# State space loop of a two-layer decoder: where a batch's x is transposed and where its y is gated

## What is computed

```python
zxbcdt = x @ W_in.T                       # z 512, xBC 768, dt 64
xBC = silu(causal_conv(xBC, conv_w))      # 4 taps
dt = softplus(dt_raw + dt_bias);  a = dt * -exp(A_log);  cum = cumsum(a)
M  = (C B^T) * exp(cum_i - cum_j) * dt_j  # lower triangle, 64 heads
y  = M @ xs + D * xs                      # 512 columns
yz = y * silu(z)                          # the gate
out = (yz * rsqrt(mean(yz^2) + eps) * norm_w) @ W_out.T
```

## Time and profile before

| | |
|---|---|
| median of 3 runs | 2280.41 us (2278.93 to 2284.31) |
| the profiled execution | 2281.86 us, its span 2279.9 us |
| busy share of the span: PE, DVE, ACT, POOL | 90%, 73%, 58%, 55% |
| state space stage | from about 923 us to 1370 us of the span |

### The profile page before, as it was taken

How to read it: one execution, slowest core, us unless ns; L and a number is a source line. 1 busy time by engine, 2 the same in 40 slices (tenths; PEclk the granted TensorE clock), 3 DMA queues, 4 the chain that set the end, 5 groups by cost and what they waited for, 6 DMA issues and landing times.

```text
span 2279.9 us, 35595 instructions
## 1 busy us (share of the span) xinstructions
PE 2049.1 (90%) x10116; PEld 1339.3 (59%) x10116; DVE 1663.0 (73%) x3833; ACT 1330.4 (58%) x5022; POOL 1256.0 (55%) x1508
## 2 busy tenths in 40 slices
PE   7889999999999996698989985999999999999996
PEld 5646666566665663455555542666666666666664
DVE  7755666676666765688887764777878788878886
ACT  3655666666666664233333224777777777777773
POOL 0153444544445431377766662667676777777775
PEclk9989999999999999799999987999999999999998
DMA  6000000000000010100000002000000000000000
GB/s 214 1 19 3 3 4 2 5 2 2 2 2 5 0 56 23 66 19 19 19 19 10 1 0 81 3 4 6 6 6 7 6 5 6 5 6 5 6 3 8
DMA packets 30094, 37.61 MB, mean 16 GB/s; under 512 B 3329, under 2 KB 24321, under 8 KB 29313
## 3 DMA queue, kind: packets, MB, share of 16 engines
q1 hardware_dynamic: 29952, 36.11, 4.8%
HBM read 34.00 MB, written 2.10 MB: 16 GB/s over the span
## 4 chain that ended last, share of the span: by engine, by line
PE 66%; DVE 12%; ACT 12%; issue 7%; POOL 3%; DMA 0%; DVEq 0%; SPq 0%; POOLq 0%; ACTq 0%
PE xa_pJB L715 5%; PE xa_pS L734 5%; PE ssm_pX L1289 5%; PE fa_pJB L1774 5%; PE xa_pO L808 5%; PE xa_pY L838 5%; PE xa_pJA L715 4%; PE fa_pS L1793 4%; PE ssm_pL L1283 3%; PE fa_pY L1824 3%; PE fa_pJA L1754 3%; PE fa_pO L1811 3%; PE fa_pH L1875 2%; DVE ssm_y L1532 2%; PE fa_pJB L1754 2%
## 5 line engine op out<-in xcount | busy, mean ns | idle before, releaser
L1242 POOL TENSOR_TENSOR ssm_y<-ssm_y,ssm_term 128x512 f32<-128x512 f32 x112 | 141.9, 1267 | 120.8 <-DVE ssm_term L1485 118.5
L1710 POOL TENSOR_TENSOR fa_rs<-fa_rs,all_minus_half 128x4 f32<-128x4 f32 x192 | 198.2, 1032 | 15.1
L1901 ACT ACTIVATE fa_qT<-fa_pH,all_fa_head_vec 128x512 f32<-128x512 f32 x128 | 99.5, 777 | 172.3 <-PE fa_pH L1875 172.3
L1910 ACT ACTIVATE fa_pS<-fa_pS,fa_nb 128x128 f32<-128x128 f32 x512 | 182.6, 392 | 7.2 <-issue 6.8
L1707 POOL TENSOR_TENSOR fa_rs<-fa_ms,all_eps5w 128x4 f32<-128x4 f32 x192 | 43.9, 229 | 240.0 <-ACT fa_q_junk L1894 132.3
L1793 PEld LDWEIGHTS fa_pS<-fa_kT,fa_qT 128*128 128x128 f32 x1024 | 124.7, 192 | 65.3 <-ACT fa_qT L1901 58.5
L1733 POOL TENSOR_TENSOR fa_cat<-fa_ov,fa_om 128x512 bf16<-128x512 f32 x128 | 153.7, 1201 | 5.3
L667 POOL TENSOR_TENSOR xa_rs<-xa_ms,all_eps 128x4 f32<-128x4 f32 (+1 forms) x65 | 13.1, 201 | 259.3 <-ACT xa_junk L882 259.3
L1793 PE MATMUL fa_pS<-fa_kT,fa_qT 128*128 128x128 f32 x1024 | 149.1, 289 | 2.4 <-ACT fa_qT L1901 0.9
L1724 POOL TENSOR_TENSOR fa_ov<-fa_ob,fa_om 128x512 f32<-128x512 bf16 x128 | 147.8, 1154 | 4.7 <-DVE fa_om L2088 4.7
L734 PE MATMUL xa_pS<-all_shared_weights,xa_qT 128*128 128x256 f32 x512 | 125.8, 387 | 23.3 <-ACT all_shared_weights L913 17.5
(11 more groups left out here) (327 smaller groups left out, 5944.3 us busy)
## 6 DMA issues: line engine op xcount, KB each, us to landing
all_shared_weights<-in_fa_w SPq DMA_DIRECT2D x12, 512.0 KB, 3.8
fa_cat<-in_fa_wproj SPq DMA_DIRECT2D x8, 512.0 KB, 3.8
all_shared_weights<-in_xa_wq SPq DMA_DIRECT2D x1, 2048.0 KB, 14.0
xa_wo<-in_xa_wo SPq DMA_DIRECT2D x1, 2048.0 KB, 18.8
xa_ctxT<-in_ctxT SPq DMA_DIRECT2D x16, 128.0 KB, 2.1
all_shared_weights<-in_fa_wkvx SPq DMA_DIRECT2D x1, 2048.0 KB, 8.7
fa_ctxT<-in_ctxT SPq DMA_DIRECT2D x16, 128.0 KB, 2.1
out_x<-all_X SPq DMA_DIRECT2D x16, 128.0 KB, 1.7
```

The lines of the kernel that those rows point to most:

```text
L1710: pool.tensor_tensor(rs[:, j % 2, cols], rs[:, j % 2, cols], env.mhalf[:, cols], ALU.pow)\
L1910: last = act.activation(four(pS[j % 2])[:, i, :], four(pS[j % 2])[:, i, :], ACT.Exp, bias=nb[:, j % 2, i:i + 1], accum_out=rsum[:, j % 2, ...
```

## The change

Four moves, all in `state_space`.

- PE: the transposes of x of batch m+1 are issued in step m, behind the last tap and ahead of the spans matmuls. Batch 0's are issued ahead of the wait for the stage's weights.
- ACT: the copy to `xT` of batch m+1 is issued in step m, between the silu of xs and the exp of the decays. Batch 0's is issued ahead of the steps.
- DVE: the gate of batch m-1 is issued in step m, behind term 6, with a wait for the POOL addition of level 6; before, it was the first instruction of step m+1.
- DVE: the residual (1517) has a further wait, for the normalised x of the batch before.

```diff
     def tensor(pe):
+        def transpose_x(b):
+
+            pe.wait_ge(s["z_in"], now(b, 0))
+            for k in range(KT):
+                last = pe.transpose(pZ[:, k * P:(k + 1) * P], env.X[:, b, k * P:(k + 1) * P], env.ident[:])
+            last.then_inc(s["xT_ps"], 1)
+
...
             if front:
-                pe.wait_ge(s["z_in"], now(m, 0))
-                for k in range(KT):
-                    last = pe.transpose(pZ[:, k * P:(k + 1) * P], env.X[:, m, k * P:(k + 1) * P], env.ident[:])
-                last.then_inc(s["xT_ps"], 1)
                 pe.wait_ge(s["xT_in"], now(m + 1, 0))
...
             if front:
                 last.then_inc(s["xs_ps"], 1)
+                if m + 1 < B:
+                    transpose_x(m + 1)
                 pe.wait_ge(s["a_done"], now(m + 1, 0))
...
         env.xa_stage.left(pe)
+        transpose_x(0)
         pe.wait_ge(w_ready, 1)
...
+        def copy_x(b):
+
+            act.wait_ge(s["xT_ps"], now(b + 1, 0))
+            act.activation(xT[:, :, PAD:PAD + P], pZ[:, 0:D].rearrange("p (k c) -> p k c", k=KT),
+                           ACT.Copy).then_inc(s["xT_in"], 1)
+
...
             if front:
-                act.wait_ge(s["xT_ps"], now(m + 1, 0))
-                act.activation(xT[:, :, PAD:PAD + P], pZ[:, 0:D].rearrange("p (k c) -> p k c", k=KT),
-                               ACT.Copy).then_inc(s["xT_in"], 1)
...
                 act.activation(xs[:], pX[:, :], ACT.Silu).then_inc(s["xs_in"], 1)
+                if m + 1 < B:
+                    copy_x(m + 1)
                 act.wait_ge(s["dec_ps"], now(m + 1, 0))
...
         act.wait_ge(pad_in, 1)
+        copy_x(0)
         sequences(act, steps)
...
-            if back:
-                dve.wait_ge(y_added, now(m - 1, 0, LEVELS, LEVELS - 1))
-                dve.tensor_tensor(y[:, 1 - side, :], y[:, 1 - side, :], sz[:, 1 - side, :], ALU.mult)\
-                    .then_inc(s["gated"], 1)
             if front:
...
                 dve.wait_ge(s["rms_done"], now(m - 1, 0))
+                dve.wait_ge(norm.x_done, now(m - 1, 0) - 1)
...
             terms(6)
+            if attend:
+                dve.wait_ge(y_added, now(m, 0, LEVELS, LEVELS - 1))
+                dve.tensor_tensor(y[:, side, :], y[:, side, :], sz[:, side, :], ALU.mult).then_inc(s["gated"], 1)
             if front:
```

## The result

The changed kernel takes 2274.68 us (median of 16 runs, 2271.67 to 2278.80) against 2281.09 us (16 runs): 6.4 us less, ratio 0.9973 with a 95% interval of 0.9965 to 0.998. So it is faster, by 4.6 to 8.0 us. The forecast was 4.8 us less. The execution that the profile shows took 2278.80 us, its span 2276.9; it is the slowest of the 16, and its state space stage begins 2.5 us later than in the profile before, for reasons that lie ahead of the stage.

What follows compares the result with a forecast made beforehand. The prediction took the ACT, DVE, ACT, PE loop of each state space batch as the bound. Copies +5.70, gates -7.80 and -0.86, start and end terms gave -4.76 us: 2280.41 - 4.8 = 2275.6, range 2272.2 to 2280.2.

Steps and rivals of the forecast that it cites:

- The loop: State space batch, from decays ready to the next decays ready: ACT to DVE, DVE, ACT, PE sets its time.
- Part 1, the gate: DVE: moving the gate takes 0.60 us a batch out of the loop; xdt, blocked by skip, ends at 1132.97.
- with nothing to spare: DVE against ACT: blocked xdt, ending at 1132.97, is just covered by dec, ready at 1132.98.
- Part 2, the copy: ACT: the copy to xT pushes table load and dec by 0.38 us a batch and buys nothing.
- the sum: Whole change: 5.70 - 7.80 - 0.86 + 0.27 - 0.60 - 0.87 - 0.60 = -4.76 us.
- 7.80 - 0.86: DVE: 13 gates at 0.60 us save 7.80; the first gate, stuck behind a POOL centring, saves 0.86.
- Part 3, the start: Batch 0 on PE: dt starts at most 1.20 us earlier, at half clock, taken as 0.60 us saved.
- The terms at the end: Stage end on DVE: batch 14's gate -0.60, batch 15's gate -0.87, late xdt in batch 15 +0.27 us.
- The second rival: POOL's power operation holds the gate on DVE, 15 x 0.32 = 4.8 us, gain gone, 2280.4; chance 0.15.
- The third: PE clock: rises after the same work, another 0.60, and a fall costing 1.6 vanishes, -7.0 us, 2273.4; chance 0.17.
- The fourth: PE clock falls behind the new stop ahead of level 2, 1.6 us each, +6.4 us, 2286.8; chance 0.06.

Runs made afterwards that it cites:

- runs 10 to 12: Second profiles of the kernel before, the changed kernel, and the kernel with the gate moved and skip on DVE: 2280.61, 2275.06 and 2272.73 us.
- run 2: Only the gate moved against the kernel before, x transposed and copied in its own step: 2274.77 us, ratio 0.9971.
- run 4: Full change plus, in the gate's old place on DVE, a multiply of the same size that nobody reads: 2290.25 us, ratio 1.0037 to the kernel before.
- run 5: Kernel before with the gate moved and skip computed on DVE behind xdt instead of on POOL, x as before: 2271.31 us, ratio 0.9957.
- runs 1 and 4: Run 1: only x transposed and copied ahead, gate left in its old place, 2288.40 us, ratio 1.0032 to the kernel before; run 4 has its own line.

## Why the prediction was right

**The loop** was right and was what decided. All experiments gave the steady batch that it asks for within 0.04 us, down to 25.23, once the copy's 0.27 and the late `xdt`'s 0.29 were known from the changed kernel. The prediction itself asked for 0.22 less a batch; it was 0.32.

**Part 1, the gate.** 0.60 out of the loop, as worked out. `xdt` blocked by `skip`, as worked out: it was to end 2.22 behind the last addition (1132.97 against 1130.75) and did so by 2.20 (1133.34 against 1131.14). The margin "with nothing to spare" turned out the other way round by 0.08: `xdt` comes last, behind `dec`, and holds `xd`.

**Part 2, the copy.** The mechanism was right (in ACT's way, buys nothing), the term mis-sized. I counted its duration, 0.38; it moves the table load and `dec` by 0.27, since it starts 0.10 ahead of the end of xs, 1131.04 against 1131.14, where a table load doesn't. That is the term that was off: the sum has 15 x 0.38 = +5.70, and with the blocked `xdt` as the true releaser it is 15 x 0.29 = +4.35. The difference of 1.35 us takes the forecast from -4.8 to -6.1. The stage without its costly falls of the clock is 6.0 and 6.1 us shorter in the two pairs of profiles (runs 10 to 12), and the stretch between the first and the last xs alone is 4.3 and 4.2 us shorter, where 4.35 - 7.80 - 0.86 gives -4.31. I had seen from the rows that both delays are of one size, but not that this makes the copy's half of the change worthless: with the gate alone the 0.29 is paid as well.

**Part 3, the start.** From the stage's first DVE instruction to the first xs 24.35 us before and 24.15 after, in the second pair 24.33 and 23.72: -0.2 and -0.6. The forecast had -0.60. dt does start 1.24 us earlier in the stage, as against the 1.20 worked out, and the B and C part of batch 0 takes 6.0 to 6.4 us now instead of 5.4, since more of it is done at half speed. The granted clock rises 13.4 us into the stage in both profiles before, 14.3 and 13.5 us into it with the change; run 2, which starts as before does, has 14.4 and takes 24.81. So this term moves by some half a microsecond from profile to profile, and that 0.60 came out in the second is in part luck. Its reason was wrong, too: the stretch of half speed doesn't begin with PE's first work at 930.83. The granted clock in the kernel before is 0.50 from 915 us on already (columns as in the earlier trace rows):

```profile
915.00:920.00 5.00, 2.67 (x16) 1.82 (x16) 1.12 (x2) 2.31 (x2) 0.00 (x0) 0.50 0.00 0
925.00:930.80 5.80, 0.00 (x0) 0.00 (x0) 5.76 (x9) 0.00 (x0) 0.00 (x0) 0.50 0.81 274
```

**The terms at the end:** -0.60 - 0.87, and `xdt` late by 0.27 for batch 15. From the start of the last xs to the end of the stage's last normalised x it is 29.60 before and 28.18 after, in the second pair 29.69 and 28.43: -1.4 and -1.3 where the three give -1.2.

**The second rival** (POOL's power operation holds the gate) is out: the gate takes 0.69 (0.691 to 0.693) in the 15 batches with the operation beside it, and 0.691 in the first, which has none. The Trainium skill's rule (SBUF — State Buffer, section Who interferes with whom) holds for `skip` against `xdt` and for both `xd`; for this operation with one element per partition the measurement decides, and it doesn't block. **The third** didn't hold up: the fall that cost 1.3 us in batch 13 before (1269 to 1277) is missing in the first profile with the change, but it is missing in the second of before as well, and others came in its place; nor did the second 0.6 at the start come. **The fourth**: the stop did move ahead of level 2, and B and C parts at a lowered clock were more frequent; these stand ahead of the new slack and cost nothing in the steady batches. But a fall behind the new stop is real. The second profile of the changed kernel has one, at a stop of 3.64, and it costs 1.5 us, near the 1.6 of the rival:

```profile
1270.51 2.05 PE L1290 MATMUL ssm_pL<-ssm_xd,ssm_cb 128*128 128x512 f32 x2 [3.64 <-DVE ssm_term L1497]
```

Level 2 takes 2.05 instead of 1.10. Behind the steady stops of 1.7 us there was none in either profile; in run 4 both of the 2.3 us ones have one.

## What to carry to other kernels

Close the loop before pricing a wait: a stop on the busiest engine is slack if the engine that releases its next step isn't through either. Price a move by when the next thing behind it starts, and where two delays meet in one `max`, test each half of a change alone; here one half carries all of it, and the other is a loss as soon as its cover goes. Where the rows show two operations of DVE and POOL one after the other, as the two `xd` here, add their times, and give the work to the faster one.

## What the runs showed of the hardware that I had not expected

- A copy on ACT behind a silu starts 0.10 us ahead of the silu's end (1131.04 against 1131.14), so in front of a table load it costs 0.27 and not its 0.38.
- DVE's `xd` of 3072 elements takes 3.36 us, 1.07 for two more levels; POOL's last level alone takes 0.92 once the way is free. DVE does a level in little more than half of POOL's time (0.53 against 0.92), and the two exclude each other, in whichever order they start: POOL ends 2.72 behind DVE when DVE is first, DVE 2.15 behind POOL when POOL is (run 5).
- Falls of the granted clock on PE, with B and C taking 5.4 instead of 3.79 us, were 11 in 16 batches in runs 1 and 4, 8 and 6 in the two profiles of the changed kernel, 5 and 3 in those of the kernel before. What sets their number stays open.
